# A Mamba-and-experts layer on one core: fewer short VectorE operations, and another order of the shared PSUM bank

## The reference, cut to what matters

```python
x = x + layernorm(mamba(layernorm(x)))          # first half: "e", "f" and the state steps
x = x + layernorm(ffn(layernorm(x)))            # second half: "p" (up to the routing), experts, "z"

def mamba(x):                                    # d_model 256, d_inner 512, d_state 16, 4 taps
    xb, z = split(rms_norm(x) @ in_proj_w)       # xb: 512 channels, z: 512 channels
    xc = silu(conv4(xb) + conv_b)                # along time
    dt, Bm, Cm = split(xc @ x_proj_w)            # 1, 16, 16 columns
    dt = softplus(dt @ dt_proj_w + dt_proj_b)
    h = exp(dt * A) * h + dt * Bm * xc           # along time, per channel and state
    y = (sum over states of h * Cm) + xc * D
    return (y * silu(z)) @ out_proj_w + x

def ffn(x):                                      # 16 experts of width 128, 4 groups of 4
    scores = sigmoid(x @ gate_w); choice = scores + e_bias
    # a group's score: the sum of its two largest; the best 2 groups stay
    # the best 4 experts of these; ties go to the lower index
    w = scores of the 4 / (their sum + 1e-20)
    return sum over experts of w * down(silu(gate(x)) * up(x))
```

## Time and profile before

| | |
|---|---|
| median of 3 runs | 2657.78 us (2655.29 to 2659.5) |
| the profiled execution | 2660.87 us, of which the span is 2659.1 us |
| TensorE busy | 2385.4 us, 90% |
| VectorE busy | 2418.0 us, 91% |
| ScalarE busy | 1606.2 us, 60% |
| GpSimd busy | 1495.1 us, 56% |
| mean granted TensorE clock | 0.957 of full speed |

### The profile page before, as it was taken

One profiled execution on the slowest core, in us unless ns is written; L12 is line 12 of the kernel. 1 busy time (PEld: TensorE's weight loads), 2 busy tenths in 40 slices (PEclk: granted clock), 3 DMA queues, 4 the chain that ended last, 5 costly groups with the idle time before them and its releaser, 6 DMA issues.

```text
span 2659.1 us, 26874 instructions
## 1 busy us (share of the span) xinstructions
PE 2385.4 (90%) x8416; PEld 1187.2 (45%) x8416; DVE 2418.0 (91%) x3097; ACT 1606.2 (60%) x3186; POOL 1495.1 (56%) x531
## 2 busy tenths in 40 slices
PE   5546899999989999898999989899999989898987
PEld 2112354544545454454545445454544545443554
DVE  4989999999999999999999999999999999999542
ACT  6556566665665666666665666666666665644331
POOL 0555565656555565656666565656656565665521
PEclk9768899999999999999999999999999999998999
DMA  4441433525353352534345253534435353442221
GB/s 144 155 145 50 161 130 116 175 87 188 106 154 119 118 183 88 188 108 151 123 133 166 87 188 111 159 112 138 161 94 181 114 161 100 147 149 84 80 71 58
DMA packets 172762, 344.50 MB, mean 130 GB/s; under 512 B 16044, under 2 KB 81357, under 8 KB 164173
## 3 DMA queue, kind: packets, MB, share of 16 engines
q1 hardware_dynamic: 164700, 334.93, 37.5%
q0 software_dynamic: 7920, 7.87, 2.2%
HBM read 291.35 MB, written 51.38 MB: 129 GB/s over the span
## 4 chain that ended last, share of the span: by engine, by line
PE 64%; DVE 20%; ACT 11%; issue 5%; DMA 1%; POOL 0%; SPq 0%; ACTq 0%; DVEq 0%; POOLq 0%
PE Gp L483 13%; PE MY L501 12%; PE Up L491 12%; DVE hs L1033 10%; PE FP L408 7%; PE Y L515 6%; DVE hs L1019 5%; PE FP L446 4%; PE FP L420 3%; PE FP L428 2%; ACT dA L591 2%; ACT XB L684 1%; ACT L591 1%; PE Y L512 1%; DVE th L1148 1%
## 5 line engine op out<-in xcount | busy, mean ns | idle before, releaser
L911 POOL TENSOR_TENSOR hs<-hs,Cb 128x2048 f32<-128x2048 f32 x256 | 1159.5, 4529 | 174.9 <-DVE hs L1019 174.9
L591 ACT ACTIVATE dA<-dtr,A 128x512 f32<-128x512 f32 x1024 | 696.7, 688 | 603.2 <-DVE hs L1033 601.8
L896 POOL TENSOR_TENSOR th<-th,cmb 128x512 f32<-128x512 f32 x256 | 325.5, 1275 | 945.8 <-DVE hs L1019 851.3
L1033 DVE TENSOR_TENSOR_SCAN hs<-dA,carry,hs 128x512 f32<-128x512 f32 x512 | 630.7, 1269 | 13.7 <-ACT dA L591 12.8
L1033 DVE TENSOR_TENSOR_SCAN hs<-dA,hs 128x512 f32<-128x512 f32 x512 | 598.8, 1208 | 37.5 <-ACT dA L591 37.0
L483 PE MATMUL Gp<-x2T,Wgu 128*128 128x512 f32 x1024 | 534.3, 646 | 82.2 <-DVE th L1143 81.6
L1019 DVE TENSOR_TENSOR hs<-dxr,Bb 128x2048 f32<-128x2048 f32 x256 | 587.8, 2296 | 6.9 <-DMA dxr<-dx_d 6.9
L491 PE MATMUL Up<-x2T,Wgu 128*128 128x512 f32 x1024 | 491.6, 603 | 0.0
L501 PE MATMUL MY<-Wdn,th 128*128 128x256 f32 x2048 | 484.4, 380 | 1.6 <-POOL th L896 1.6
L501 PEld LDWEIGHTS MY<-Wdn,th 128*128 128x128 f32 x2048 | 384.3, 190 | 135.1 <-issue 89.8
L483 PEld LDWEIGHTS Gp<-x2T,Wgu 128*128 128x128 f32 x1024 | 183.5, 198 | 420.0 <-issue 275.6
(11 more groups left out here) (168 smaller groups left out, 1798.5 us busy)
## 6 DMA issues: line engine op xcount, KB each, us to landing
dxr<-dx_d SPq DMA_DIRECT2D x128, 512.0 KB, 7.2
dtr<-dt_d SPq DMA_DIRECT2D x64, 1024.0 KB, 5.5
cmb<-cm_d SPq DMA_DIRECT2D x256, 256.0 KB, 3.6
Wdn<-in_w_dn SPq DMA_DIRECT2D x256, 128.0 KB, 3.4
Bb<-bc_d SPq DMA_DIRECT2D x64, 256.0 KB, 3.0
Cb<-bc_d SPq DMA_DIRECT2D x64, 256.0 KB, 3.6
dt_d<-XB SPq DMA_DIRECT2D x15, 1024.0 KB, 4.3
dx_d<-DX SPq DMA_DIRECT2D x15, 1024.0 KB, 5.8
```

The costliest lines, as they stand in the source:

```text
L591: act.activation(dA[h % 2][:, :], dtr[:, M % 2, beta, :], ACT.Exp, scale=A[:, k:k + 1]).then_inc(s_dA, 1)
L896: pool.tensor_tensor(th[:, q % NTH, :], th[:, q % NTH, :], cmb[:, q % 2, :], ALU.mult).then_inc(m_a, 1)
L911: pool.tensor_tensor(hs[:, G % NH, :, :], hs[:, G % NH, :, :], Cb[:, s, :].unsqueeze(1).broadcast_to([P, NBETA, CH]), ALU.mult).then_inc(s ...
L1033: dve.tensor_tensor_scan(hv, dA[h % 2][:, :], hv, first, ALU.mult, ALU.add).then_inc(s_h, 1)
```

## The change

It has three parts.

1. **Fewer short operations on VectorE.** The inverse square root starts with one operation where two stood, and has two steps, the first of a higher order (5 operations), the second as before (3): 8 in a chain where 11 were. The norms' numbers lie side by side (`n_sq`, `n_v`, `n_rs`, `n_nb`), so that one variance and one factor operation serve several norms. In the routing the "+1" moves to ScalarE (a second short operation in `p_sig`), and comparisons, masks and sums are merged; one operation is added (`oke`). The 1e-20 becomes a constant column of `picked`.
2. **Another order of the bank FP.** k2 and k3 move from g 1 and g 5 ahead of the expert's down product to g 0 and g 4 behind it; z0 from g 4 to g 5; z1 from g 6 to g 10; z2 from g 9 to g 11, z3 from g 9 to g 11; db stays in g 9, now ahead of the down product. ScalarE reads k3 in the middle of g 5, z0 at its end, z1 in the middle of g 11, z2 at its end, z3 in the middle of g 12.
3. **The experts' squares in the next chunk.** For chunks 0 to 13 `z_squares` moves from g 13 to the middle of g 3 of the next period, `z_norm` from g 10 to the middle of g 5, the adding DMA from g 11 to g 10. Chunks 14 and 15 stay where they were.

```diff
-FILLS = ['b2', 'k2', 'r0', 'r1', 'b3', 'z0', 'k3', 'z1', 'xp', 'x0', 'x1', 'rt', 'z2', 'z3', 'db', 'ct', 'xT0', 'xT1', 'b0', 'b1']
+FILLS = ['b2', 'k2', 'r0', 'r1', 'b3', 'k3', 'z0', 'xp', 'x0', 'x1', 'rt', 'db', 'ct', 'z1', 'z2', 'z3', 'xT0', 'xT1', 'b0', 'b1']
...
TensorE, ahead of the expert's down product:
-                if F and g in (0, 4, 6, 9):
-                    f_in(p, {0: 'b2', 4: 'b3', 6: 'z1', 9: 'z2'}[g])
-                if F and g in (1, 5):
-                    f_conv(p, PE_CONV[g // 4])
+                if F and g in (0, 4, 5, 11):
+                    f_in(p, {0: 'b2', 4: 'b3', 5: 'z0', 11: 'z2'}[g])
+                if F and g == 9:
+                    f_dt(p)
...
TensorE, behind it:
-                if F and g == 4:
-                    f_in(p, 'z0')
-                if F and g == 9:
-                    f_in(p, 'z3')
-                    f_dt(p)
+                if F and g in (0, 4):
+                    f_conv(p, PE_CONV[g // 4])
+                if F and g in (10, 11):
+                    f_in(p, {10: 'z1', 11: 'z3'}[g])
...
ScalarE:
                 act.activation(R[:, 0, :], FP[:, 0:TB * NE], ACT.Exp, scale=-1.0).then_inc(p_act.sem, 1)
+                act.wait_ge(p_act.sem, p_act.at(c, 'ex'))
+                act.activation(R[:, 0, :], R[:, 0, :], ACT.Copy, bias=1.0).then_inc(p_act.sem, 1)
...
-                if F and g == 7:
-                    f_z(p, 1)
+                if F and g == 5:
+                    f_tap(p, PE_CONV[1])
+                if F and g in (11, 12):
+                    f_z(p, {11: 1, 12: 3}[g])
...
-                if g == 10 and 0 <= p - 3 < NC - 2:
+                if g == 3 and 0 <= p - 3 < NC - 2:
+                    z_squares(p - 3)
+                if g == 5 and 0 <= p - 3 < NC - 2:
                     z_norm(p - 3)
-                if g == 12 and NC - 2 <= p - 2 < NC or g == 13 and 0 <= p - 2 < NC - 2:
+                if g == 12 and NC - 2 <= p - 2 < NC:
                     z_squares(p - 2)
...
-                if F and g in (1, 5):
-                    f_tap(p, PE_CONV[g // 4])
+                if F and g == 1:
+                    f_tap(p, PE_CONV[0])
...
-                if F and g == 4:
+                if F and g == 5:
                     f_z(p, 0)
...
                 if F and g == 9:
-                    f_z(p, 2)
-                    f_z(p, 3)
                     f_softplus(p)
...
+                if F and g == 11:
+                    f_z(p, 2)
...
GpSimd:
-                if g == 11 and 0 <= p - 3 < NC - 2:
+                if g == 10 and 0 <= p - 3 < NC - 2:
                     add_out(p - 3)
...
VectorE, the inverse square root (it replaces the one with three equal steps):
+            def newton(steps, c, tag, v, y, a):
+                def done(name):
+                    dve.wait_ge(steps.sem, steps.at(c, f'{tag}_{name}'))
+                dve.tensor_scalar(y.bitcast(I32), v.bitcast(I32), -0.5, RSQRT_MAGIC, ALU.mult, ALU.add).then_inc(steps.sem, 1)
+                done('guess')
+                dve.scalar_tensor_tensor(out=a, in0=y, scalar=-RSQRT_K, in1=y, op0=ALU.mult, op1=ALU.mult).then_inc(steps.sem, 1)
...
+                dve.scalar_tensor_tensor(out=y, in0=a, scalar=1.875, in1=y, op0=ALU.add, op1=ALU.mult).then_inc(steps.sem, 1)
...
VectorE, the norms of g 4 in one function:
+                if E:
+                    dve.wait_ge(e_act.sem, e_act.at(i, 'sq'))
+                    dve.tensor_scalar(n_v[:, 0:TB], n_sq[:, 0:TB], (1.0 + RMS_EPS) / DM, LN_EPS * RMS_EPS, ALU.mult, ALU.add).then_inc(n_dve.sem, 1)
+                if Z:
+                    dve.wait_ge(z_act.sem, z_act.at(p - 3, 'sq'))
+                if R_:
+                    dve.wait_ge(p_act.sem, p_act.at(p - 1, 'sq'))
+                v0 = max(c0, TB)
+                variance(n_v[:, v0:c1], n_sq[:, v0 - TB:c1 - TB]).then_inc(n_dve.sem, 1 if E else 2)
+                dve.wait_ge(n_dve.sem, n_dve.at(i, 'var'))
+                newton(n_dve, i, 'r', n_v[:, c0:c1], n_rs[:, i % 4, c0:c1], n_a[:, c0:c1])
+                dve.tensor_tensor(n_nb[:, i % 4, c0:c1], n_nm[:, i % 4, c0:c1], n_rs[:, i % 4, c0:c1], ALU.mult).then_inc(n_dve.sem, 1)
...
VectorE, the routing:
-                dve.tensor_scalar(den, den, 1.0, None, ALU.add).then_inc(p_dve.sem, 1)
...
-                dve.tensor_tensor(tb, pair[:, :, 0], pair[:, :, 1], ALU.max).then_inc(p_dve.sem, 1)
...
-                dve.tensor_tensor(gg, gg, ge, ALU.add).then_inc(p_dve.sem, 1)
...
-                dve.tensor_scalar(gm, gr, float(TOPG), None, ALU.is_lt).then_inc(p_dve.sem, 1)
+                dve.scalar_tensor_tensor(out=t4, in0=gr.unsqueeze(2).broadcast_to([P, NGB, NE // NG]), scalar=float(TOPG), in1=q4, op0=ALU.is_lt, op1=ALU.mult).then_inc(p_dve.sem, 1)
...
-                dve.tensor_tensor(per_b(cs), per_b(cs), wide(ng), ALU.add).then_inc(p_dve.sem, 1)
...
+                dve.tensor_tensor(eq, cs, eq, ALU.mult).then_inc(p_dve.sem, 1)
...
-                dve.tensor_scalar(ws, ws, 1e-20, None, ALU.add).then_inc(p_dve.sem, 1)
```

More of the change, by code:

```diff
@@ L70, in rsqrt_names @@
 def rsqrt_names(tag):
-    return [f'{tag}_half', f'{tag}_guess'] + [f'{tag}_{s}{n}' for n in range(3) for s in ('a', 'b', 'y')]
+    return [f'{tag}_{s}' for s in ('guess', 'a0', 't0', 'q0', 'y0', 'a1', 't1', 'y1')]
 class Steps:
@@ L143, in sandwich_kernel @@
         SZ = sb('SZ', [P, 2, MT, CH])
[L144 to L147, removed]
+        e_s = sb('e_s', [P, TB])
+        n_sq = sb('n_sq', [P, 3 * TB])
+        n_v = sb('n_v', [P, 4 * TB])
+        n_a = sb('n_a', [P, 4 * TB])
+        n_nm = sb('n_nm', [P, 4, 4 * TB])
+        n_rs = sb('n_rs', [P, 4, 4 * TB])
+        n_nb = sb('n_nb', [P, 4, 4 * TB])
         dtr = sb('dtr', [P, 2, NBETA, CH])
@@ L164, in sandwich_kernel @@
         comb = sb('comb', [P, TB * NE])
+        picked = sb('picked', [P, TB, NE + 1])
         th = sb('th', [P, NTH, CH])
@@ L619, in e_sums @@
                 act.wait_ge(ld_xin, 16 * (c + 1))
-                sums(xin, e_s).then_inc(e_act.sem, 1)
+                for b in range(TB):
+                    ins = act.activation(xin[:, b, :], xin[:, b, :], ACT.Copy, accum_out=e_s[:, b:b + 1])
+                ins.then_inc(e_act.sem, 1)
             def e_squares(c):
@@ new lines, in variance, with norms @@
+            def variance(v, sq):
+                return dve.tensor_scalar(v, sq, 1.0 / DM, LN_EPS, ALU.mult, ALU.add)
+            def norms(p):
+                i = p + 2
+                E, R_, Z = (i < NC, in_p(p), 0 <= p - 3 < NC - 2)
+                c0, c1 = (0 if E else 2 * TB, (4 if Z else 3 if R_ else 2) * TB)
+                if E:
[10 more added lines that the diff above has]
+                dve.tensor_tensor(n_nb[:, i % 4, c0:c1], n_nm[:, i % 4, c0:c1], n_rs[:, i % 4, c0:c1], ALU.mult).then_inc(n_dve.sem, 1)
@@ L1065, in _ @@
             bg = before_g.rearrange('p (i j) -> p i j', i=NG).unsqueeze(1).broadcast_to([P, TB, NG, NG])
-            gg, ge = (R[:, k, :].rearrange('p (b i j) -> p b i j', b=TB, i=NG) for k in (7, 0))
+            over = flat[:, 5 * TB * NE:7 * TB * NE].rearrange('p (b i k j) -> p b i k j', b=TB, i=NG, k=2)
+            gg, ge = (over[:, :, :, k, :] for k in range(2))
             t4 = tmp.rearrange('p (g e) -> p g e', e=NE // NG)
@@ L1070, in _ @@
             fourth = top8[:, :, TOPK - 1]
-            ng, ws, wr = (R[:, 7, k * TB:(k + 1) * TB] for k in range(3))
-            sel = den
+            nle, ws, wr = (R[:, 7, k * TB:(k + 1) * TB] for k in range(3))
+            chosen = picked[:, :, 0:NE]
             def route_groups(p):
@@ L1109, in done @@
                     dve.wait_ge(p_dve.sem, p_dve.at(c, name))
-                done('gm')
-                dve.tensor_tensor(t4, q4, gm.unsqueeze(2).broadcast_to([P, NGB, NE // NG]), ALU.mult).then_inc(p_dve.sem, 1)
                 done('tmp')
```

212 lines of the change are left out of this document (86 added, 126 removed).

## The result

The changed kernel takes 2587.29 us (median of 4 runs, 2586.42 to 2588.29), beside 2658.5 us for the kernel before on the same chip (2655.29 to 2659.5). The ratio is 0.9734, 95% interval 0.972 to 0.9748: 71 us faster. The prediction was 2597, with a range of 2578 to 2632.

What follows compares the result with a forecast made beforehand. It took VectorE to bound the kernel. Part 1's 39 us, 9 us in the first two chunks and 13 of 22 us of steady waits made 61 us: 2600 from the profiled 2660.9, 2597 as median, range 2578 to 2632.

Steps and rivals of the forecast that it cites:

- The likeliest case: Whole kernel: 61 us less, 2600 against the median 2597; own range 2583 to 2613; chance 62%.
- Part 1, 39 us of work: Short VectorE operations in g 4, 6 and 9: 2.4 us a chunk, 39 us in all, bounds 30 and 44.
- a sign of ScalarE being too full: A new VectorE wait in g 4, 6 or 12 of over 0.5 us in each chunk would show the forecast wrong.
- I take VectorE as the bound: Steady chunks: TensorE has time left in g 11, VectorE none, so an operation or wait less on VectorE shortens the chunk.
- Part 2, the waits: Steady chunks, g 1, 2, 5, 8, 10, 15: 22 us of waits can go, 60% counted, 13 us.
- The first two chunks, 9 us of waits: p = 0 and 1: in g 10 1.6 of 7.63 us stay, 1.9 in g 8 and 1.0 go; together 9 us.
- TensorE gains it, VectorE nothing: g 13: ScalarE hands the transposes over about 1 us sooner; part 3 costs nothing, or up to 0.8 us a chunk.
- g 13's wait stays: VectorE's wait of 0.85 us in g 13, from silu_z with its table loads, stays.
- The waits come back: Rival: scaling and squares push ScalarE, each costing VectorE 0.5 to 1 us a chunk; 2616, or 2630; chance 16%.
- TensorE becomes the bound: Rival: TensorE's other idle time stays, so a chunk couldn't fall below about 153 us; 2635; chance 8%.
- More than forecast: Rival: removed unlinked operations save the skill page's price (8 us), and all 22 us of waits go; 2580; chance 8%.
- Slower: Rival: k3 over 5 us late in g 5 in all chunks stalls ScalarE; 2672 at 6 us late; chance 4%.

Runs made afterwards that it cites:

- part 1 alone: The kernel before with only fewer short VectorE operations, the bank's order and the squares' place as before: 2650.66 us, ratio 0.997.
- part 2 alone: The kernel before with only the new order of the shared bank FP: 2638.07 us, ratio 0.9924.
- part 3 alone: The kernel before with only the experts' squares in g 3 and scaling in g 5 of the next chunk: 2646.82 us, ratio 0.9959.
- parts 1 and 3: The changed kernel with the old order of the bank put back: 2638.63 us, ratio 0.9934 to the kernel before.
- parts 1 and 2: The changed kernel with the squares back in g 13 and the scaling in g 10: 2594.38 us, ratio 0.9763 to the kernel before.
- z half, parts 1 and 3: The changed kernel with k2, k3 and z0 back in g 1, g 5 and g 4; z1, z2, z3 and dt row as changed: 2593.85 us.
- the z half alone: The kernel before with only z1 filled in g 10, z2 and z3 in g 11, the dt row ahead of g 9's down product: 2639.62 us.
- the kernel with eight unlinked operations: The changed kernel plus eight 4-column VectorE operations in g 9, writing different tiles with no semaphore between them: 2593.65 us, ratio 0.9762 to the kernel before.
- the kernel that moves the gating: The changed kernel with ScalarE's gating of z moved from g 12 to g 2 of the next period: 2574.53 us, ratio 0.9692 to the kernel before.
- without the z half: The changed kernel with z1 back in g 6, z2 and z3 in g 9, copied ahead of the softplus; k2, k3, z0 as changed: 2639.15 us.
- eight operations more on VectorE: The changed kernel plus eight 4-column VectorE operations in g 9, each waiting by semaphore for the one ahead: 2611.06 us, ratio 0.9831 to the kernel before.

## Why the prediction was right, and where it was wrong

The likeliest case came true, 10 us better than forecast and within its own range. By place, the 61 us that were counted and the 74.5 us by which the span fell are:

| | counted | measured |
|---|---|---|
| head | 0.8 | 3.3 |
| p = 0 and 1 | 12.2 | 7.8 |
| p = 2 to 14 | 44 | 60.3 |
| p = 15 and the tail | 3.9 | 3.1 |

That the time is near is in part luck: the step on what bounds the kernel was wrong, and what made up for it was the other part of the same change. Step by step:

| | VectorE busy | waits for decays, tanh, Y | sum | span |
|---|---|---|---|---|
| part 1 alone | -39.4 | +32.3 | -7.1 | -10.3 |
| part 2 alone | -1.6 | -19.9 | -21.5 | -22.5 |
| part 3 alone | -2.5 | -8.2 | -10.7 | -10.5 |
| parts 1 and 3 | -39.5 | +21.9 | -17.6 | -22.6 |
| parts 1 and 2 | -40.9 | -20.0 | -60.9 | -61.9 |
| z half, parts 1 and 3 | -41.8 | -24.4 | -66.2 | -69.2 |
| the change | -42.5 | -29.1 | -71.6 | -74.5 |

Each is the difference to the kernel before in one profiled execution, in us: from the pages, and from the three totals of each list of waits. Head and tail stand in it as well. Other waits (for the variances, and 1.8 us for Y ahead of an `inputs` in the changed kernel) and the gaps too short to be listed are left out, which is why sum and span differ. With all of them the change is -42.5, -24.4 (all listed waits) and -7.6 (short gaps), together -74.5; part 1 alone is -39.4, +36.6 and -7.5, together -10.3.

- **Part 1, 39 us of work: right in size.** VectorE's busy time fell by 39.4 us with part 1 alone; in the changed kernel g 4 gave 0.90 (0.9 predicted), g 9 1.01 (0.9). The operations ahead of the third variance turned into waiting as said: 0.57 to 0.60 us there in every steady chunk. I had named a wait of over 0.5 us in g 4 as a sign of ScalarE being too full; with part 1 alone, which gives ScalarE only one short operation a chunk more, the wait is the same, so here it was no such sign.
- **"I take VectorE as the bound": wrong of the kernel before.** The step reasoned from TensorE's idle time in g 11. But g 11 is where the two meet; from g 14 to g 9 TensorE had no gap, all that part 1 removes in a steady chunk, in g 4, 6 and 9, lies in that stretch, and ScalarE tied the two by its copies of the z's. Part 1 alone brought 8 us, not 39, and 1.9 of the 31 counted for p = 2 to 14. The chain, TensorE 64%, had it right. The statement became true by the other part of the same change, which is why the time came out.
- **Part 2, the waits: right, and the discount wrong.** The waits in g 2, 5, 8 and 10 of the steady chunks all went, 22 us; I counted 60%, 13. This is the term that was mis-sized, by 9 us: without the discount the forecast would have been 2588. The waits of g 6 (3.9 us), which I kept, went as well; against them stand 4 us more at the variance in g 4. (In the list of waits g 13 should have stood at 12.8 us, not 13.6; no term used it.) What I did not see is that the z half alone is most of part 2 and decides whether part 1 pays.
- **The first two chunks, 9 us of waits and some 3 of part 1: too much.** They gave 8 us in all. The waits of 7.63 and 1.9 went as said, but waits for Y came (1.81 us in g 13 of p = 0, 1.97 in g 1 of p = 1). In part these only take back the early start of the scans: the kernel with eight unlinked operations has the same order of the bank, starts its scans at 52.4 us and not at 50.1, has no wait for Y in g 13 and 0.58 us in g 1, and begins p = 1 at 179.7 us, the changed kernel at 180.0. The z half with parts 1 and 3 begins p = 2 at 318.2 us, the changed kernel at 321.1. So k2, k3 and z0 in their new places may cost 1 to 3 us here; this is not shown, they were not tried one by one.
- **Part 3, "TensorE gains it, VectorE nothing": wrong.** It is worth 12 us alone, and 7 in the change (2594.38 to 2587.29, with intervals that touch). Its covers held: no wait for ScalarE in g 3 or 5 of the steady chunks. What I had left out is what TensorE's microsecond in g 14 does later. First the kernel without part 3, then the changed one, TensorE's waits for the transposes:

```profile
PE FP L398 <- ACT xT L630: 32.9, 14, 8.5
```

```profile
PE FP L398 <- ACT xT L630: 23.8, 14, 8.3
```

  TensorE's waits there are 9 us shorter in all, about 1 us in an even chunk and 0.2 in an odd one, and VectorE's waits for Y ahead of its gating product in g 1 and g 5, 11.5 us without part 3, are 3.5 us.
- **g 13's wait stays: right** (0.75 to 0.84 us), and the kernel that moves the gating gains 13 us, with these waits gone.
- **The rivals.** "The waits come back" is what happens without the z half, though not by the new blocks on ScalarE that I named. "TensorE becomes the bound" failed, but the 153 us that were to tell it were worked out wrong: 147.3 us of work and 4 idle, or 154.8 less the 3.6 of g 11, are 151.2, and 151.2 is what p = 7 now takes. What speaks against it is that TensorE is idle for 4.7 us of it (146.55 of 151.20), 2.15 of them waiting for VectorE, that the even chunks fell to 148.6, and that eight operations more on VectorE arrive in the time nearly in full. "More than forecast" (2580) was right in its second half, all waits gone, and wrong in its first, the price of unlinked operations. "Slower" needed k3 to be over 5 us late in g 5; in the steady chunks from p = 4 on ScalarE waits for it 0.44 to 0.50 us in every second one and found it ready in the others.

The slack explains the pattern of the table. In a stretch in which two engines run side by side and meet at its end, the time is the longer of the two. Before, TensorE's was longer by VectorE's waits there, 2.2 us in an even chunk. Part 1 shortens the shorter one by 2.5 us: next to nothing but longer waits. Part 2 takes three fills out of the longer one, and their copies out of the way between the two: it gains until VectorE is the longer. Both together gain both.

## What to carry to other kernels

An engine that waits a little at several places in a stretch is not the one that sets its time, however busy it is: follow the thing it waits for through the engine between (here ScalarE's copies) to the one that has no gap, and count a saving on the waiting engine as nothing there until the other has been relieved by more than those waits. Add up busy time and waits of one engine in each version: if a saving on it turns up as waits of equal size, move load off the other engine first. When two parts relieve two sides of such a pair, their gains alone say little about their gain together (8, 21 and 12 us alone, 71 together).
